# Triangle products: another order of product units, dense steps, statistics and copies on four engines

## What is computed

```python
q = (x_in @ Wq).reshape(B, N, N, H, d_k)          # the same for k, v1, v2
scores = jnp.einsum('bilhd,bljhd->biljh', q, k) / np.sqrt(d_k)
att = jax.nn.softmax(scores, axis=2)
out = jnp.einsum('biljh,bilhd,bljhd->bijhd', att, v1, v2)
attn_out = out.reshape(B, N, N, E) @ Wo
h = _layer_norm(x_in + attn_out, ln_agg_g, ln_agg_b)
h = jax.nn.relu(h @ W1 + b1) @ W2 + b2 + h
return _layer_norm(h, ln_out_g, ln_out_b)
```

## Time and profile before

| | before |
|---|---|
| median of 3 runs | 5632.52 us (5631.88 to 5634.49) |
| profiled execution, its own time | 5635.91 us |
| span of the profiled execution | 5634.2 us |
| mean granted TensorE clock | 0.949 |
| busy: TensorE, weight loads | 4920.7, 4186.9 us |
| busy: VectorE, ScalarE, GpSimd | 3681.9, 2477.8, 2234.4 us |
| first triangle layer | 0 to 1672 us |
| global attention | 1672 to 3640 us |
| second triangle layer | 3640 to 5436 us |
| convolution | 5436 to 5634 us |

### The profile page before, as it was taken

One profiled execution on the slowest core, in us unless ns is written; L12 is line 12 of the kernel. 1 busy time (PEld: TensorE's weight loads), 2 busy tenths in 40 slices (PEclk: granted clock), 3 DMA queues, 4 the chain that ended last, 5 costly groups with the idle time before them and its releaser, 6 DMA issues. The chain is left out here.

```text
span 5634.2 us, 212039 instructions
## 1 busy us (share of the span) xinstructions
PE 4920.7 (87%) x87968; PEld 4186.9 (74%) x87968; DVE 3681.9 (65%) x6141; ACT 2477.8 (44%) x6232; POOL 2234.4 (40%) x1165
## 2 busy tenths in 40 slices
PE   7888888888877999999789999979888879888867
PEld 6677776677764799999569999967777767777756
DVE  3677763777764566666546666644777754777767
ACT  5555545555532333333233333326555536555533
POOL 0677760777755000000320000000777741777730
PEclk9999999999988999999899999989999989999988
DMA  2000002000002000000110000011000011000012
GB/s 78 20 19 20 20 17 67 18 20 19 20 24 90 19 14 14 14 14 14 61 44 14 14 14 17 14 38 54 18 20 20 19 37 46 20 20 20 19 44 86
DMA packets 183274, 162.65 MB, mean 29 GB/s; under 512 B 23216, under 2 KB 178480, under 8 KB 183088
## 3 DMA queue, kind: packets, MB, share of 16 engines
q1 hardware_dynamic: 183088, 160.07, 9.4%
HBM read 109.66 MB, written 50.33 MB: 28 GB/s over the span
## 5 line engine op out<-in xcount | busy, mean ns | idle before, releaser
L810 POOL TENSOR_TENSOR tri_work<-tri_v,tri_work 128x1024 f32<-128x1024 f32 x768 | 1807.0, 2367 | 595.7 <-PE tri_psum L566 595.2
L724 DVE TENSOR_TENSOR tri_work<-tri_v,tri_psum 128x1024 f32<-128x1024 f32 x1280 | 1505.4, 1217 | 251.4 <-PE tri_psum L566 236.4
L566 PE MATMUL tri_psum<-tri_work 128*32 128x64 f32 x65536 | 1211.2, 230 | 273.9 <-DVE tri_work L724 252.9
L566 PEld LDWEIGHTS tri_psum<-tri_work 128*32 128x32 f32 x65536 | 1048.2, 117 | 490.0 <-DVE tri_work L724 402.1
L1216 ACT ACTIVATE global_work<-global_psum 128x512 f32<-128x512 f32 x512 | 306.2, 598 | 1059.1 <-PE global_psum L1164 1059.1
L1300 POOL TENSOR_TENSOR global_work<-global_work,global_bp 128x256 f32<-128x256 f32 x64 | 46.1, 738 | 1677.5 <-DVE global_work L1282 1670.4
L1257 DVE TENSOR_REDUCE global_work<-global_work 128x1 f32<-128x512 f32 x512 | 349.3, 682 | 503.7 <-ACT global_work L1216 503.7
L1184 PE MATMUL global_psum<-global_v_high,global_pT_high 128*128 128x256 f32 x2048 | 616.7, 301 | 2.7 <-DVE global_pT_low L1275 2.7
L1184 PE MATMUL global_psum<-global_v_low,global_pT_high 128*128 128x256 f32 x2048 | 577.5, 282 | 0.0
L1184 PE MATMUL global_psum<-global_v_high,global_pT_low 128*128 128x256 f32 x2048 | 577.5, 282 | 0.0
L1164 PE MATMUL global_psum<-global_k_high,global_q_high 128*128 128x512 f32 x1024 | 422.8, 413 | 23.0 <-DVE global_q_low L1238 21.6
(11 more groups left out here) (136 smaller groups left out, 7913.1 us busy)
## 6 DMA issues: line engine op xcount, KB each, us to landing
tri_work<-in_x SPq DMA_DIRECT2D x192, 128.0 KB, 2.1
tri_work<-x SPq DMA_DIRECT2D x192, 128.0 KB, 2.1
x<-tri_work SPq DMA_DIRECT2D x128, 128.0 KB, 1.7
tri_work<-in_x SPq DMA_DIRECT2D x128, 64.0 KB, 2.2
global_work<-x SPq DMA_DIRECT2D x16, 512.0 KB, 4.2
xn<-global_work SPq DMA_DIRECT2D x16, 512.0 KB, 3.3
qT<-global_work SPq DMA_DIRECT2D x32, 256.0 KB, 2.1
global_work<-qT SPq DMA_DIRECT2D x64, 128.0 KB, 2.2
```

The lines of the kernel that those rows point to most:

```text
L566: mm = nc.tensor.matmul(psum[32 * g:32 * g + 32, OW, region * N:region * N + N], v1_diag[:, c * 32:c * 32 + 32], src[:, at_ * N:at_ * N + ...
L724: nc.vector.tensor_tensor(prod_d[k % 2].rearrange("p (d j) -> p d j", d=CU), v2[:, c:c + CU, :], psum[:, A[n.slot], (c // D) * N:(c // D + ...
L810: nc.gpsimd.tensor_tensor(prod_p[k % 2].rearrange("p (d j) -> p d j", d=CU), v2[:, c:c + CU, :], a_sb[n.slot][:, h * N:(h + 1) * N].unsque ...
```

## The change

The order of the work within a body changes, on TensorE, ScalarE and VectorE; GpSimd's own order stays and only the places of its units in TensorE's order change. Each engine has the same instructions as before.

- `UNITS` becomes DDDPDPDDPPDDDPPD: the P units stand at 3, 5, 8, 9, 13 and 14 instead of 2, 5, 7, 10, 13 and 15.
- TensorE: wo after two units instead of three; w2 after four instead of six; the pair transposes after ten instead of eight; v1 after eleven instead of nine and now ahead of the a transposes, which move from after eight units to after eleven; the hn transposes after thirteen instead of eleven.
- ScalarE: the square root moves from behind the copies of a to directly behind the exps, ahead of the pair's copy.
- VectorE: the statistics of h0 move ahead of the reciprocal and the probabilities. Product 5 moves ahead of the aggregates and the variance, product 7 ahead of the inverse root, product 8 between the inverse root and hn, product 9 between hn and on. None is left behind on.

```diff
-            UNITS = "DDPDDPDPDDPDDPDP"
+            UNITS = "DDDPDPDDPPDDDPPD"
...
                         if units:
                             unit(n, 0)
                             unit(n, 1)
-                            unit(n, 2)
                         if dense:
...
                             mm.then_inc(s["wo_mm"], 1)
                         if units:
+                            unit(n, 2)
                             unit(n, 3)
-                            unit(n, 4)
-                            unit(n, 5)
                         if last:
...
                             mm.then_inc(s["w2_mm"], 1)
                         if units:
-                            unit(n, 6)
-                            unit(n, 7)
+                            for u in range(4, 10):
+                                unit(n, u)
                         if prep:
                             pe.wait_ge(s["pair_in"], slot_after_each(nxt))
                             pe.wait_ge(s["v1_high"], after(nxt - 1))
                             for k in range(KC):
                                 mm = nc.tensor.transpose(psum[:, V, k * P:k * P + P], x_pair[:, k * P:k * P + P], eye)
                             mm.then_inc(s["pairT_mm"], 1)
-
+                        if units:
+                            unit(n, 10)
+                        if prep:
+                            pe.wait_ge(s["pairT_copy"], after(nxt))
+                            for k in range(KC):
+                                mm = nc.tensor.matmul(psum[:, V, E:2 * E], x_pairT[:, k * P:k * P + P], wv1[:, k, :],
+                                                      start=(k == 0), stop=(k == KC - 1))
+                            mm.then_inc(s["v1_mm"], 1)
+                        if prep:
                             pe.wait_ge(s["probs_ready"], after(nxt))
...
                             mm.then_inc(s["a_mm"], 1)
                         if units:
-                            unit(n, 8)
-                        if prep:
-                            pe.wait_ge(s["pairT_copy"], after(nxt))
-                            for k in range(KC):
-                                mm = nc.tensor.matmul(psum[:, V, E:2 * E], x_pairT[:, k * P:k * P + P], wv1[:, k, :],
-                                                      start=(k == 0), stop=(k == KC - 1))
-                            mm.then_inc(s["v1_mm"], 1)
-                        if units:
-                            unit(n, 9)
-                            unit(n, 10)
+                            unit(n, 11)
+                            unit(n, 12)
                         if dense:
                             pe.wait_ge(s["hn_ready"], after(prv))
...
                         if units:
-                            for u in range(11, NU):
+                            for u in range(13, 16):
                                 unit(n, u)
...
                             ins.then_inc(s["exp_ready"], 1)
+                        if dense or last:
+                            act.wait_ge(s["variance"], after_root(n, 1, 1))
+                            nc.scalar.activation(root, variance, ACT.Sqrt).then_inc(s["root"], 1)
                         if prep:
                             act.wait_ge(s["pairT_mm"], after(nxt))
...
                                                  ).then_inc(s["a_copy"], 1)
-                        if dense or last:
-                            act.wait_ge(s["variance"], after_root(n, 1, 1))
-                            nc.scalar.activation(root, variance, ACT.Sqrt).then_inc(s["root"], 1)
...
                         if units:
                             unit(n, 4)
+                        if dense:
+                            dve.wait_ge(s["h0_ready"], after(prv))
+                            nc.vector.bn_stats(stats1, h0).then_inc(s["stats1"], 1)
                         if prep:
                             dve.wait_ge(s["exp_ready"], after(nxt))
...
-                        if dense:
-                            dve.wait_ge(s["h0_ready"], after(prv))
-                            nc.vector.bn_stats(stats1, h0).then_inc(s["stats1"], 1)
                         if last:
                             dve.wait_ge(s["w2_mm"], after(old))
                             nc.vector.bn_stats(stats2, psum[:, X, 0:E]).then_inc(s["stats2"], 1)
+                        if units:
+                            unit(n, 5)
                         if dense:
                             dve.wait_ge(s["stats1"], after(prv))
...
                         if units:
-                            unit(n, 5)
                             unit(n, 6)
+                            unit(n, 7)
                         if dense or last:
...
                             dve.wait_ge(s["rstd"], after_root(n, 5))
+                        if units:
+                            unit(n, 8)
                         if dense:
                             nc.vector.tensor_scalar(hn, h0, mv1[:, 0:1], rstd[:, 0:1], ALU.subtract, ALU.mult
                                                     ).then_inc(s["hn_ready"], 1)
+                        if units:
+                            unit(n, 9)
                         if last:
...
                                                     ).then_inc(s["on_ready"], 1)
-                        if units:
-                            for k in range(7, ND):
-                                unit(n, k)
```

More of the change, by code:

```diff
@@ L734, in body @@
                         if units:
-                            for k in range(4):
-                                unit(n, k)
+                            for u in range(0, 4):
+                                unit(n, u)
                         if dense:
@@ L818, in body @@
                         if units:
-                            for k in range(NPL):
-                                unit(n, k)
+                            for u in range(0, 6):
+                                unit(n, u)
                         if last:
```

## The result

| | before | after |
|---|---|---|
| median | 5632.71 us (5631.88 to 5634.49, 4 runs) | 5331.34 us (5328.91 to 5337.39, 4 runs) |
| profiled execution, its own time / span | 5635.91 / 5634.2 us | 5331.34 / 5329.7 us |
| mean granted clock over the span | 0.949 | 0.963 |

The ratio is 0.9466, 95% interval 0.945 to 0.9483: 301 us faster. The forecast was 5325, with a range of 5285 to 5412.

The account below looks back on a forecast made before the run. The prediction took a chain passing between engines, ending in VectorE's wait for the root, as the bound. From 5635.9 it took 288 us for 116 intervals and 20 for edges, then 3.4 to the median: 5325 us, range 5285 to 5412.

Parts of the forecast that it names:

- u0: First of TensorE's sixteen units in a pair interval, time 0 of the forecast timetable; the next one at 17.95 us.
- D5: VectorE's product 5 (counted from 0) in a pair interval, forecast to run from 7.07 to 8.29 us.
- u7: TensorE unit 7 (counted from 0), forecast to wait for D5 and start at 8.34 us, 0.6 late.
- u9: TensorE unit 9 (counted from 0), forecast to start at 9.97 us after GpSimd's product, the wait that ends last.
- u12: TensorE unit 12 (counted from 0), forecast to start at 13.56 us, using D8.
- D8: VectorE's product 8 (counted from 0), forecast from 12.3 to 13.5 us, hidden by about 0.05 only.
- 2.04 of chain and 0.44 of clock: Forecast gain per pair interval, 20.48 to 18.0 us: shorter chain between engines plus no low-clock stretches; 288 us over 116.
- Rival B: Low-clock stretches stay in the pair intervals, one each 40.96 us, costing 78 us: 5403 us, chance 0.08.
- twelve edge bodies: The other full pair steps of the four blocks, claimed to gain 0 to 30 us in all, taken as 20.
- C: VectorE becomes the bound, through late D8 or hn or D5 delaying the statistics: 5370 to 5440 us, chance 0.12.
- D: No gain: GpSimd's product P3, waiting for a TensorE unit, replaces the root wait entirely; 5630 us, chance 0.02.
- E: Slower: TensorE's clock falls for long in each pair interval; 6.5 us low give some 5665 us, chance 0.03.

Follow-up runs that it names:

- e5: Changed kernel with one GpSimd unit moved ahead of one VectorE unit in TensorE's order (UNITS DDDPPDDDPPDDDPPD): 5367.07 us.
- e6: Changed kernel with w2 on TensorE after six units instead of four: 5384.58 us.
- e10: Kernel before with filler identity products added in TensorE's waits, written to a bank whose content is used up: 5588.0 us.
- e1: Kernel before with only ScalarE's square root moved ahead of the pair's copy: 5473.1 us.
- e2: Kernel before with only VectorE's new order of statistics and products: 5655.77 us.
- e3: Kernel before with only TensorE's new order and the new UNITS: 6260.48 us.
- e4: Changed kernel with the square root put back behind the copies of a on ScalarE: 6046.49 us.

## Why the prediction was right

**What bounds the kernel.** The chain a copies, table load, root, inverse root, hn, products was the binding one: taking the root out of it alone gave 0.93 per interval at full clock as worked out (20.00 to 19.07), and putting it back on the changed kernel made VectorE wait 4.46 at the same place. The account of TensorE's waits lacked the 0.47 ahead of u8; the forecast did not need it, since it was added up from a new timetable and not from waits taken off.

**The timetable.** After u0 it had: D5 7.07 (measured 7.08), u7 8.34 (8.35), u9 9.97 (10.00), v1 11.50 (11.53), u12 13.56 (13.50), hn transposes 14.12 (14.06), w1 15.97 (15.91), next u0 17.95 (17.88). Variance was forecast for 8.9, it ends at 8.73. D8 was forecast at 12.3 and starts at 12.03, so the cover (the time by which a step is ready ahead of its use) was 0.25 for D8 and 0.35 for hn, not 0.05 to 0.1; the two runs that spent it (e5, e6) found its end. 2.48 per interval in 116 intervals was 288; measured 298.4, since the interval came out at 17.91 where I had rounded up to 18.0.

**The clock.** The forecast split the 2.48 into 2.04 of chain and 0.44 of clock. The low stretches of the interiors went entirely, and e10 prices them at 51 us, 0.44 per interval. Rival B, that they stay, is excluded: the kernels here have none, or one in each second, third, fourth or every interval, according to TensorE's waits. The rule of the Trainium skill, "TensorE: Matmul & The Clock Gate", section "Why this matters for your kernels", which asks for no gap above some 3 us, is not enough here: the longest gap of before was 1.14 us. The measurement decides. The granted clock says more than one gap does: e1 keeps waits of 0.47, 1.05 and 0.48 and has a clock of 1.00, e2 has one of 2.55 and fewer low stretches than the kernel before.

**The edges.** Here a size was off: twelve edge bodies and all the rest were taken at 20 us and gave 6. Inside the blocks, first to last product of VectorE, the edges did gain: the four blocks shrink by 309 us, 11 more than the interiors. But the entry got longer, by an item that the sum did not have. The first timelines show a block's start, before and after:

```profile
173.44 0.20 DVE L746 RECIPROCAL tri_small<-tri_small 128x8 f32<-128x8 f32 x1 [2.74 <-ACT tri_psum L660]
...
175.43 1.91 PE L620 MATMUL tri_psum<-tri_wv,tri_work 128*128 128x256 f32 x4
...
176.65 2.35 DVE L724 TENSOR_TENSOR tri_work<-tri_v,tri_psum 128x1024 f32<-128x1024 f32 x2 [2.19 <-ACT tri_psum L675]
```

```profile
174.66 0.20 DVE L747 RECIPROCAL tri_small<-tri_small 128x8 f32<-128x8 f32 x1 [2.75 <-ACT tri_psum L658]
...
177.25 1.06 PE L619 MATMUL tri_psum<-eye,tri_work 128*128 128x128 f32 x4
...
178.53 0.33 ACT L675 ACTIVATE tri_work<-tri_psum 128x192 f32<-128x192 f32 x1 [3.19 <-PE tri_psum L619]
...
179.33 3.65 DVE L722 TENSOR_TENSOR tri_work<-tri_v,tri_psum 128x1024 f32<-128x1024 f32 x3 [3.65 <-ACT tri_psum L676]
```

From the last exps' reciprocal (173.44 before, 174.66 after) to the first product it is 3.2 us before and 4.7 after: in the body that only prepares, the a transposes now stand behind v1, and no unit of a pair covers that. The runs bear it out: this stretch is 3.2 in all four blocks of every run with TensorE's old order, and 4.5 to 4.8 in every run with the new one, e3 among them. Four times 1.46 are 5.8 us. In the first block the clock is 0.50 there for 13.65 us after the change and for 6.83 before.

That the total came out within 6 us of the forecast is in part luck: the interiors gave 10 more than the sum had, the edges 14 less.

**The other rivals.** C (VectorE late) and D (P3 takes the root's place) did not occur in the changed kernel; C is what e5 and e6 show. E, slower by a falling clock, did not occur; e3 and e4 show the mechanism with its price.

## What to carry to other kernels

When no engine fills the period of a loop, write the timetable of one period from the trace and see who waits last; the edits of several engines' orders are then one change, and one of them alone can cost more (626 us here) than all together gain (301). A table load or another fixed cost belongs behind the event that is ready earliest, not behind a copy at the end of another chain. Count for each step that is moved how much cover it has left, and for each period the granted clock beside the waits: here waits of 0.82 and 1.14 us, close together, cost another 0.44 per interval through the clock.

## What I had not expected

Adding 1.35 us of useless products per interval to the kernel before made it 46 us faster. The period of before also looks tied to its low stretches: the two intervals around one take 20.01 and 20.95, together 40.96, which is the distance from one low stretch to the next; without them the pair takes 40.05. That the stretches set the period, and do not just follow it, is not shown by any run. And the size of the interaction between the parts: +626 us for TensorE's order alone, the same order that is part of a 301 us gain.
